# A root shared between ScalarE and VectorE, and three small moves, in a conditional adapter with layer norm

## The reference

```python
Wd = W_down[stream]; bd = b_down[stream]; Wu = W_up[stream]; bu = b_up[stream]
g = ln_w[stream];    b = ln_b[stream]
h = einsum('bsh,bhk->bsk', x, Wd) + bd[:, None, :]     # x is (4, 512, 512), k is 256
h = gelu(h, approximate=False)
h = einsum('bsk,bkh->bsh', h, Wu) + bu[:, None, :]
h = x + h
mean = mean(h, -1); var = mean((h - mean)**2, -1)
out = (h - mean) * rsqrt(var + 1e-5) * g[:, None, :] + b[:, None, :]
```

## Time and profile before

| | |
|---|---|
| median of 3 runs | 66.01 us (65.88 to 66.51) |
| the profiled execution | 66.02 us |
| its span in the profile | 64.3 us, so 1.72 us lie around it |
| PE busy | 55.3 us, 86% |
| DVE busy | 51.7 us, 80% |
| POOL busy | 44.1 us, 69% |
| ACT busy | 33.5 us, 52% |
| granted TensorE clock | 0.98 over the span |

### The profile page before, as it was taken

The page is one execution under the profiler, slowest core; times in us unless marked ns, Lnnn a source line. Parts: engine busy times, 40 slices in busy tenths (PEclk is TensorE's granted clock), DMA queues, the critical chain, the costliest instruction groups (busy, mean ns, idle before and its releaser), DMA issues. The chain is left out here.

```text
span 64.3 us, 916 instructions
## 1 busy us (share of the span) xinstructions
PE 55.3 (86%) x254; PEld 44.5 (69%) x254; DVE 51.7 (80%) x101; ACT 33.5 (52%) x53; POOL 44.1 (69%) x52
## 2 busy tenths in 40 slices
PE   0999999995999999999999999999999999980000
PEld 0979835873888888887888888788998889640000
DVE  0039999999099999979999997999999999999400
ACT  0070033969993019999910799990169772604000
POOL 5600007099879989998999899899988083493700
PEclk9999999999999999999999999999999999999975
DMA  0899999998999999999999999561001605244090
GB/s 0 265 386 194 297 301 387 384 431 347 410 448 416 405 418 410 418 443 386 409 410 413 420 441 403 224 278 79 0 10 48 283 0 217 110 163 163 0 331 0
DMA packets 5058, 17.92 MB, mean 279 GB/s; under 512 B 694, under 2 KB 694, under 8 KB 4668
## 3 DMA queue, kind: packets, MB, share of 16 engines
q1 hardware_dynamic: 4608, 16.80, 66.8%
q10 hardware_dynamic: 444, 1.06, 4.7%
HBM read 13.66 MB, written 4.19 MB: 278 GB/s over the span
## 5 line engine op out<-in xcount | busy, mean ns | idle before, releaser
L273 POOL TENSOR_TENSOR x_lo<-x_raw,x_hi 128x512 fp32r<-128x512 f32 x10 | 12.8, 1299 | 0.8 <-ACT x_hi L355 0.8
L709 PE MATMUL y_ps<-wu_hi,hid_lo 128*128 128x512 f32 x32 | 12.1, 400 | 0.7 <-DVE hid_lo L466 0.7
L676 PE MATMUL y_ps<-wu_hi,hid_hi 128*128 128x512 f32 x32 | 12.5, 395 | 0.0
L683 PE MATMUL y_ps<-wu_lo,hid_hi 128*128 128x512 f32 x32 | 12.2, 390 | 0.0
L284 POOL TENSOR_TENSOR wu_lo<-w_raw,wu_hi 128x512 fp32r<-128x512 f32 x8 | 10.9, 1361 | 1.7 <-ACT wu_hi L365 1.7
L477 DVE BATCH_NORM_STATS2 stats<-y_ps 128x6 f32<-128x512 f32 x16 | 10.5, 686 | 1.8 <-PE y_ps L683 1.8
L494 DVE SCALAR_TENSOR_TENSOR y_ps<-y_ps,mean_var,ln_gb 128x512 f32<-128x512 f32 x16 | 11.4, 748 | 0.0
L504 DVE SCALAR_TENSOR_TENSOR result<-y_ps,rstd,ln_gb 128x512 f32<-128x512 f32 x13 | 9.4, 739 | 0.1
L377 ACT ACTIVATE hid_hi<-hid_ps,w_raw 128x512 fp32r<-128x512 f32 x6 | 4.1, 688 | 9.3 <-PE hid_ps L637 8.2
L289 POOL TENSOR_TENSOR rstd<-var_eps,minus_half 128x2 f32<-128x2 f32 (+1 forms) x10 | 6.4, 640 | 2.7 <-DVE var_eps L485 2.7
L629 PE MATMUL hid_ps<-x_hi,wd_hi 128*128 128x512 f32 x20 | 8.2, 409 | 0.0
(11 more groups left out here) (51 smaller groups left out, 103.0 us busy)
## 6 DMA issues: line engine op xcount, KB each, us to landing
x_raw<-x_cols SPq DMA_DIRECT2D x6, 512.0 KB, 8.9
x_raw<-x_rows SPq DMA_DIRECT2D x3, 1024.0 KB, 10.8
out<-result SPq DMA_DIRECT2D x6, 512.0 KB, 4.7
w_raw<-weights SPq DMA_DIRECT2D x4, 512.0 KB, 9.4
ln_gb<-ln_rows SPq DMA_DIRECT2D x4, 512.0 KB, 13.4
w_raw<-weights SPq DMA_DIRECT2D x3, 516.0 KB, 11.6
x_raw<-x_cols ACTq DMA_DIRECT2D x2, 512.0 KB, 3.8
out<-result SPq DMA_DIRECT2D x4, 256.0 KB, 2.3
```

The lines of the kernel that those rows point to most:

```text
L273: nc.gpsimd.tensor_tensor(x_lo[:, b % 2, k, :], x_raw[:, b, k, :], x_hi[:, b % 2, k, :].bitcast(F32), ALU.subtract).then_inc(x_lo_done, 1)
L676: nc.tensor.matmul(y_ps[:, t, :], hid_hi[:, p, j, t * P:(t + 1) * P], wu_hi[:, p, j, :], start=False, stop=False, skip_group_check=True)
L683: product = nc.tensor.matmul(y_ps[:, t, :], hid_hi[:, p, j, t * P:(t + 1) * P], wu_lo[:, p, j, :], start=False, stop=last, skip_group_chec ...
L709: product = nc.tensor.matmul(y_ps[:, t, :], hid_lo[:, p, j, t * P:(t + 1) * P], wu_hi[:, p, j, :], start=False, stop=last, skip_group_chec ...
```

## The change

Four edits, of which two belong together:

1. The last tile's root, (3,3): POOL's `inverse_std(LAST, 3, TT)` goes. ACT loads the table set of the square root ahead of its last `scale`, and takes the square root of var_eps into a new column `last_std`; DVE takes its reciprocal into rstd behind the last `centre`, and `finish(LAST, 3)` waits for that.
2. `shift_var` adds eps to one column at a time in all batches (128x1 instead of 128x2, so twice as many in batches 0 to 2).
3. `split_x` is cut in `round_x` and `lo_x`; the low part of x of batch 1, k = 1, is made after the two `lo_hidden` of batch 0 instead of before them.
4. Tile (2,2) joins SHARED: DVE's `finish(2, 2)` is replaced by a `scale` on ACT and a `shift` on POOL, each just ahead of those of tile (2,3). SyncE's store of the tiles 2 and 3 of batch 2 waits for `shifted` alone.

```diff
-        SHARED = [(LAST - 1, 3), (LAST, 1), (LAST, 2)]
+        SHARED = [(LAST - 1, 2), (LAST - 1, 3), (LAST, 1), (LAST, 2)]
...
                     if (b, 2 * c + 1) in SHARED:
-                        sp.wait_ge(norm_done, TT * b + 2 * c + 1)
+
                         sp.wait_ge(shifted, SHARED.index((b, 2 * c + 1)) + 1)
...
+            shift(LAST - 1, 2)
             shift(LAST - 1, 3)
             inverse_std(LAST, 0, 1)
             inverse_std(LAST, 1, 2)
             shift(LAST, 1)
             inverse_std(LAST, 2, 3)
-            inverse_std(LAST, 3, TT)
             shift(LAST, 2)
...
             gelu_half(1, 0)
+            scale(LAST - 1, 2)
             scale(LAST - 1, 3)
             copy_rows(LAST, 2)
             copy_rows(LAST, 3)
             gelu_half(1, 1)
             scale(LAST, 1)
+
+            nc.scalar.preload_act_table(ACT.Sqrt)
             scale(LAST, 2)
+            act.wait_ge(var_done, TT * B)
+            nc.scalar.activation(last_std[:], var_eps[:, LAST % 2, TT - 1:TT], ACT.Sqrt).then_inc(last_std_done, 1)
...
-            def split_x(b, k):
-                p, n = b % 2, KT * b + k + 1
+            def round_x(b, k):
                 dve.wait_ge(x_in[b][k // HALF], DMA)
-                nc.vector.tensor_copy(x_hi[:, p, k, :], x_raw[:, b, k, :]).then_inc(early_x_hi_done, 1)
-                dve.wait_ge(early_x_hi_done, n)
+                nc.vector.tensor_copy(x_hi[:, b % 2, k, :], x_raw[:, b, k, :]).then_inc(early_x_hi_done, 1)
+
+            def lo_x(b, k):
+                p = b % 2
+                dve.wait_ge(early_x_hi_done, KT * b + k + 1)
                 nc.vector.tensor_tensor(x_lo[:, p, k, :], x_raw[:, b, k, :], x_hi[:, p, k, :].bitcast(F32),
                                         ALU.subtract).then_inc(early_x_lo_done, 1)
...
-            def shift_var(b, t0, t1):
-                dve.wait_ge(mean_done, TT * b + t1)
-                nc.vector.tensor_scalar(var_eps[:, b % 2, t0:t1], mean_var[:, b % 2, t0:t1, 1], EPS, None,
-                                        ALU.add).then_inc(var_done, t1 - t0)
+            def shift_var(b, t):
+                dve.wait_ge(mean_done, TT * b + t + 1)
+                nc.vector.tensor_scalar(var_eps[:, b % 2, t:t + 1], mean_var[:, b % 2, t, 1:2], EPS, None,
+                                        ALU.add).then_inc(var_done, 1)
...
             def finish(b, t):
                 p, n = b % 2, TT * b + t + 1
-                dve.wait_ge(rstd_done, n)
+                if n == TT * B:
+                    dve.wait_ge(last_rstd_done, 1)
+                else:
+                    dve.wait_ge(rstd_done, n)
...
             for k in range(KT):
-                split_x(0, k)
+                round_x(0, k)
+                lo_x(0, k)
             choose_rows()
             split_bias()
-            split_x(1, 0)
-            split_x(1, 1)
+            round_x(1, 0)
+            lo_x(1, 0)
+            round_x(1, 1)
             for j in range(JT):
                 lo_hidden(0, j)
+            lo_x(1, 1)
             for b in range(LAST):
                 tile_stats(b, 0)
                 tile_stats(b, 1)
                 moments(b, 0)
                 moments(b, 1)
-                shift_var(b, 0, 2)
+                shift_var(b, 0)
+                shift_var(b, 1)
...
                 centre(b, 2)
                 centre(b, 3)
-                finish(b, 2)
+                if (b, 2) not in SHARED:
+                    finish(b, 2)
...
             for t in range(TT):
                 tile_stats(LAST, t)
                 moments(LAST, t)
-                shift_var(LAST, t, t + 1)
+                shift_var(LAST, t)
                 centre(LAST, t)
                 if t == 1:
                     lo_hidden_half(1, 1)
                     finish(LAST, 0)
+            dve.wait_ge(last_std_done, 1)
+            nc.vector.reciprocal(rstd[:, LAST % 2, TT - 1:TT], last_std[:]).then_inc(last_rstd_done, 1)
             finish(LAST, 3)
```

More of the change, by code:

```diff
@@ L88, in conditional_adapter_kernel @@
         rstd = sb("rstd", [P, 2, TT])
+        last_std = sb("last_std", [P, 1])
         minus_half = sb("minus_half", [P, TT])
@@ L143, in conditional_adapter_kernel @@
         scaled = sem("scaled")
+        last_std_done = sem("last_std_done")
         early_x_hi_done = sem("early_x_hi_done")
@@ L159, in conditional_adapter_kernel @@
         last_norm_done = sem("last_norm_done")
+        last_rstd_done = sem("last_rstd_done")
         hid_ps_done = sem("hid_ps_done")
@@ L554, in _ @@
                 moments(b, 3)
-                shift_var(b, 2, 4)
+                shift_var(b, 2)
+                shift_var(b, 3)
                 finish(b, 0)
```

## The result

| | runs | median us | lowest to highest |
|---|---|---|---|
| before | 22 | 66.01 | 65.22 to 67.71 |
| after | 22 | 65.15 | 64.81 to 66.03 |

The ratio of after to before is 0.9908, 95% interval 0.9879 to 0.9937. The two medians lie 0.86 us apart.

What follows compares the result with a forecast made beforehand. PE was taken to bound the middle, back-to-back matmuls between an opening and a 6.60 us tail. Profiled 66.02 us, minus 0.83 for the late x_lo, plus 0.01 for the root, gave 65.2 us; range 64.9 to 65.8.

Steps and rivals of the forecast that it cites:

- The late low part of x: Opening: moving x_lo(1,1) behind batch 0's lo_hidden removes PE's stop at the first L709, 0.83 us gained.
- lead: From the opening on, PE runs ahead of the kernel before: 0.93 us at first, capped at 0.83 by wd_lo(1,1).
- Eps by single columns: DVE's eps additions as single columns: nothing on the path, only cover, with 1.0 us per batch freed from first pairs.
- The shared tile: Tile (2,2), DVE's finish replaced by ACT and POOL work: DVE's gained time becomes idle, worth nothing.
- The root: Tail, last tile's root on ACT and DVE: 0.01 us lost, bounds -0.05 to +0.20; early tile 2 worth nothing.
- The table load: ACT before its last scale: 2.02 us idle covers a 1.28 us load; by the skill's 2.66, end 0.08 later.
- (1): Rival: the lead is partly lost to late loads, POOL holds or a slow reciprocal, 65.4 to 65.7 us; chance 0.21.
- (2): Rival, opening: the moved x_lo starts behind POOL's and waits, no gain, 65.9 us with a second hold; chance 0.06.
- (3): Rival, tail: the table switch falls at the root, finish 0.9 us later, 66.1 us or 67.4 at twice the price; chance 0.04.

Runs made afterwards that it cites:

- e2: The changed kernel with x_lo(1,1) back in front of the two lo_hidden of batch 0: median 65.46 us, ratio to before 1.0023.
- e7: The kernel before with only tile (2,2) shared between ACT and POOL: median 65.93 us, ratio to before 1.0006.
- e1: The kernel before with only x_lo(1,1) moved behind the two lo_hidden of batch 0: median 65.52 us, ratio to before 0.9899.
- e4: The changed kernel with the last tile's root back on POOL: median 65.06 us, ratio to before 0.9839.
- e5: The changed kernel with eps added to two columns at a time again in batches 0 to 2: median 66.08 us, ratio to before 0.994.
- e8: The kernel before with only the last tile's root on ACT and DVE: median 66.06 us, ratio to before 0.996.
- e12: The changed kernel with tile 2 stored before tile 3, ACT's first full gelu before its up-weight rounding, and the root back on POOL: median 65.27 us, ratio 0.9975.
- e10: The changed kernel with the table load behind ACT's last scale, directly ahead of the root: median 66.08 us, ratio to before 1.0103.
- e6: The kernel before with only the single columns of eps: median 65.77 us, ratio to before 0.9983.

## Why the prediction was right, and where not

The time is right, 65.2 forecast and 65.15 measured, and so is the mechanism of the late x_lo in the pair of executions that was profiled. That the medians agree to 0.05 us is in part luck: one edit was priced too high for the average execution, another at nothing, and the two errors cancel. Point by point:

**The late low part of x.** Right in the profiled pair: a lead of 0.84 us for the 0.83 forecast, and the load of wd_lo(1,1) at 21.46 + 0.41 = 21.87 for the 21.89 forecast. x_lo(1,1) ran from 15.79 in the frame of before (15.80 forecast). POOL's next x_lo took 1.42 us instead of 1.30, so it was held by 0.12, not 0.29, and had its room. What the prediction did not say is that this is the gain of one kind of execution. It read a collision with a margin of 0.28 us (12.85 to 13.13) as a fixed part of the kernel. e2 and e7 show executions without it in the same order of instructions. Over many executions this edit thus gives less than 0.83: 0.52 in the median of e1 (six runs), 0.40 from e2 to e4, which have single columns both and differ also in the root, worth nothing there, and nothing in the median of e5.

**Eps by single columns.** The wrong step: "On the path I cost this at nothing". In the middle of the profile of before PE indeed had no wait on DVE, and in the profile of e5 neither. But in executions such as e8's a pair is held through two of POOL's instructions and PE loses 0.9 us. The price was taken from one execution, for a wait whose length differs from one execution to the next, with "up to 1.23" as its longest. Single columns end the runs over 66.2, a quarter of all with pairs, and without them the median of e5 is 0.9 us over that of after (measured apart). This filled the hole that the first point left. A small misreading lies beside it: not three but all six of the 128x2 start inside a POOL instruction, and each ends within 0.03 us of that one's end; three of them only started late in it.

**The shared tile.** Right: e7 at 1.0006. There, as in after, DVE waits for ACT ahead of the last hid_lo (0.42 us).

**The root.** Right for this order of the stores: 0.01 us lost, as forecast, with 0.20 us for the root (0.3 taken) and 0.15 for the reciprocal (0.16 taken). e4 confirms that it is worth nothing, e12 that the cause is SyncE's order, as the prediction said.

**The table load.** Covered. The section cited from the Trainium skill (ScalarE: Activation LUTs, What ACT_TABLE_LOAD costs) adds a drain to the switch, 2.66 us in all. This case's trace does not agree: in e10 the load starts 0.02 us behind the scale and the next activation 0.01 us behind the load, so here the measurement decides for 1.28 us.

**The rivals.** The lead was not lost to late loads (1), and the moved x_lo did not fall behind POOL's (2). (3) was priced at 0.9 us where e10 measured 0.74.

Open: what decides whether DVE or POOL goes first at a hand-over, and in which part of the executions of before each of the two stalls happens; only one execution of each kernel was profiled. The split of the 0.86 us between the two edits is known only roughly. Five of the 22 runs of after took 65.7 us or more, up to 66.03, and no profile shows why; late up-weights, as in e4, are one candidate.

## What to carry to other kernels

A collision between two engines that a trace shows with a margin of a few tenths of a microsecond may be a coin toss, not a fixed cost: before pricing it, ask what sets the two starts (here a landing), and look at the spread of the times. Small VectorE instructions that GpSimd can hold, as the 128x2 here, are worth replacing by forms that it doesn't hold, as the 128x1, even where the profiled execution forgives the hold. And work that becomes ready earlier gains nothing behind a queue that waits for something else first: change the order of the waits with it.

## What the runs showed of the hardware

- A VectorE instruction that GpSimd holds can lose the hand-over more than once: 2.63 us for 128x2 elements, through the end of one GpSimd instruction and the whole of two more (e8). The 128x1 form of the same operation was never held: 0.131 to 0.154 us in 16 of after, of which most start while GpSimd subtracts or adds.
- With two inputs in SBUF VectorE is held by GpSimd's subtraction, and holds it, whichever starts first: 1.67 and 1.68 us against 0.69 (before, e6), and in e7 GpSimd's pair took 3.07 us against 2.55. With one input in PSUM VectorE's took 0.68 us beside GpSimd's (e7), and GpSimd's pair 2.55 beside it (after).
- A table load of ScalarE takes 1.28 us and the next activation starts 0.01 us later (e10).
- A 128x1 square root takes 0.20 us on ScalarE, a 128x1 reciprocal 0.15 us on VectorE, no more than adding a constant.
